# The node stage's first two weight loads issued in the last head pair ahead of the store of the inverse denominators

## The reference, cut to what matters

```python
xn = _layernorm(x)                                  # x: 1250 x 768
x = x + gnn(xn, edges, W, b) + mix(xn, w_qkv, w_proj)
x = x + ffn(_layernorm(x), ...)                     # 8 experts, top-1 routing

# mix: 12 heads of 64, attention with a polynomial in place of exp
A = einsum('bhnd,bhmd->bhnm', q, k)
numerator = 1.0 + A + 0.5 * A * A
attn = numerator / numerator.sum(axis=-1, keepdims=True)
out = einsum('bhnm,bhmd->bhnd', attn, v)            # then @ w_proj

# gnn: h = xn @ W, then the sum over edges (row -> col) of h[row] * norm
```

## Time and profile before

| | us |
|---|---|
| median of 3 runs | 1134.38 |
| lowest and highest of them | 1133.22, 1134.51 |
| the profiled execution, its own time | 1134.08 |
| its span in the trace | 1132.4 |
| outside the span (1134.08 - 1132.4) | 1.68 |

### The profile page before, as it was taken

One profiled execution on the slowest core, in us unless ns is written; L12 is line 12 of the kernel. 1 busy time (PEld: TensorE's weight loads), 2 busy tenths in 40 slices (PEclk: granted clock), 3 DMA queues, 4 the chain that ended last, 5 costly groups with the idle time before them and its releaser, 6 DMA issues.

```text
span 1132.4 us, 15230 instructions
## 1 busy us (share of the span) xinstructions
PE 931.7 (82%) x5250; PEld 886.2 (78%) x5250; DVE 733.0 (65%) x1396; ACT 459.4 (41%) x678; POOL 308.5 (27%) x201
## 2 busy tenths in 40 slices
PE   3896789989989989989896779699999963399970
PEld 3896688888878878878885679699999963399960
DVE  6877269879889788789786445464445436166633
ACT  2311266666666666666665212110101020266520
POOL 2035555535646545533452000000000004100004
PEclk9998899999999999999998889899999975599995
DMA  9966433373363454498534564736252332879978
GB/s 279 321 180 151 85 49 61 37 137 60 62 112 60 85 88 60 89 198 197 116 54 107 72 155 104 167 80 154 77 154 78 95 110 53 238 232 278 282 192 272
DMA packets 143091, 152.24 MB, mean 134 GB/s; under 512 B 72205, under 2 KB 119926, under 8 KB 142024
## 3 DMA queue, kind: packets, MB, share of 16 engines
q1 hardware_dynamic: 114213, 137.46, 46.7%
q0 software_dynamic: 28432, 14.05, 9.8%
q10 hardware_dynamic: 403, 0.17, 0.1%
HBM read 105.79 MB, written 46.78 MB: 135 GB/s over the span
## 4 chain that ended last, share of the span: by engine, by line
PE 57%; DVE 15%; ACT 9%; issue 8%; DMA 7%; POOL 2%; SPq 1%; DVEq 0%; ACTq 0%; POOLq 0%
PE ps L1770 14%; PE ps L1772 13%; PE ps L1771 13%; PE ps L1156 6%; PE ps L1140 3%; ACT Ph L802 3%; PE ps L1141 3%; ACT Pf L824 2%; DVE Pl L1014 2%; DVE Ph L1012 1%; DMA rows<-oE 1%; POOL rows L1511 1%; DMA Cs<-counts 1%; PE ps L1404 1%; PE ps L1116 1%
## 5 line engine op out<-in xcount | busy, mean ns | idle before, releaser
L363 POOL DMA_INDIRECT counts<-countc,idxu x157 | 273.4, 1741 | 308.5 <-DMA counts<-countc,idxu 229.9
L1014 DVE SCALAR_TENSOR_TENSOR Pl<-Pf,Ph 125x832 fp32r<-125x832 f32 (+1 forms) x180 | 184.3, 1026 | 72.6 <-ACT Ph L802 68.5
L824 ACT ACTIVATE Pf<-ps 125x832 f32<-125x832 f32 (+1 forms) x180 | 155.8, 866 | 145.9 <-PE ps L1141 140.6
L1156 PE MATMUL ps<-Ph,vsb 125*128 125x416 f32 (+1 forms) x360 | 132.1, 367 | 9.2 <-DVE Pl L1014 8.8
L1156 PE MATMUL ps<-Pl,vsb 125*128 125x416 f32 (+1 forms) x360 | 128.0, 356 | 0.0
L1511 POOL DMA_INDIRECT rows<-XF,slots x10 | 14.8, 1480 | 341.1 <-DVE slots L1626 338.4
L1770 PE MATMUL ps<-XH,wqkH 128*128 128x416 f32 (+1 forms) x216 | 81.6, 378 | 19.9 <-DVE R L932 10.2
L1770 PE MATMUL ps<-wH,XH 128*125 128x384 f32 x240 | 84.8, 353 | 9.9 <-DVE OHL L959 5.8
L1156 PEld LDWEIGHTS ps<-Ph,vsb 125*128 125x128 f32 x360 | 68.8, 191 | 19.9 <-DVE Pl L1014 9.5
L1771 PE MATMUL ps<-wL,XH 128*125 128x384 f32 x240 | 83.3, 347 | 0.0
L1772 PE MATMUL ps<-wH,XL 128*125 128x384 f32 x240 | 82.9, 346 | 0.0
(11 more groups left out here) (235 smaller groups left out, 2130.8 us busy)
## 6 DMA issues: line engine op xcount, KB each, us to landing
Cs<-counts SPq DMA_DIRECT2D x20, 546.9 KB
w1s<-L_ffn_w SPq DMA_DIRECT2D x8, 1152.0 KB, 8.6
w2s<-L_ffn_w SPq DMA_DIRECT2D x8, 1152.0 KB, 6.5
rows<-blank SPq DMA_DIRECT2D x2, 4215.0 KB
odram<-OHL SPq DMA_DIRECT2D x12, 625.0 KB, 8.9
oS<-odram SPq DMA_DIRECT2D x10, 750.0 KB, 4.8
vdram<-VS SPq DMA_DIRECT2D x10, 672.0 KB
vsb<-vdram SPq DMA_DIRECT2D x12, 560.0 KB
```

The costliest lines, as they stand in the source:

```text
L363: pool.indirect_dma_start(out=counts, out_offset=bass.IndirectOffsetOnAxis(ap=idxu[:, c:c + 1], axis=0), in_=countc[:, c:c + 1], in_offset ...
L824: act.activation(Pf[:, i % RING, :, 0:w], ps[0:T, 2 * (i % 2):2 * (i % 2) + 2, 0:w], ACT.Square, bias=1.0).then_inc(sq_done, 1)
L1014: dve.scalar_tensor_tensor(out=p, in0=f, scalar=1.0, in1=h.bitcast(F32), op0=ALU.add, op1=ALU.subtract).then_inc(p_lo, 1)
L1156: ins = pe.matmul(ps[:, 4 + s % 2, 0:w], vsb[:, 2 * kp + t, a, :], part[:, m % RING, t, 0:w], start=(kp == 0 and t == 0 and part is Ph), s ...
```

## The change

In the last pair's branch of SP's `turn`, the wait for `g_mm` (the last use of the tile kt that `wst3` lies over) and the loads of thirds 3 and 4 move ahead of `store_inverse`. The load of third 5 stays behind `load_inverse`. No instruction of another engine is touched, and no load is added.

```diff
                 else:
+                    sp.wait_ge(g_mm, PAIRS)
+                    load_w3(sp, 3)
+                    load_w3(sp, 4)
                     store_inverse(j)
                     load_inverse(j)
-                    sp.wait_ge(g_mm, PAIRS)
-                    for wc in (3, 4, 5):
-                        load_w3(sp, wc)
+                    load_w3(sp, 5)
```

## The result

| | before | changed |
|---|---|---|
| median, us | 1135.59 (1133.22 to 1139.6, 6 runs) | 1127.02 (1124.09 to 1129.24, 6 runs) |
| span of the profiled execution, us | 1132.4 | 1126.9 |
| inverses' store issued (L685), us | 594.66 | 596.23 |
| last output store issued (L734, now L735), us | 636.84 | 631.29 |
| **distance** between these two issues, us | 42.18 | 35.06 |

The ratio of the changed kernel to the one before is 0.9923, with a 95% interval of 0.9905 to 0.9940, that is 8.7 us less, and between 6.8 and 10.8. The forecast was 8.05 us. The kernel before was measured again beside the changed one, three runs more, and its median moved from 1134.38 to 1135.59, so the ratio says more than the difference of two medians. Later medians of the changed kernel, beside other runs of the one before, were 1125.29 and 1123.84.

What follows compares the result with a forecast made beforehand. The prediction took ACT's wait for W's third 3, felt by DVE and PE, as the bound; removing 8.05 us, all other terms zero, took the median from 1134.38 to 1126.3 us, range 1124.2 to 1128.3.

Steps and rivals of the forecast that it cites:

- The wait: ACT's 8.05 us wait for W's third 3 in the last head pair goes whole; DVE's falls to 2.6 us.
- DVE sets the pace: Behind the stall the stage is as long as DVE's unaltered work, busy 19.29 of 19.60 us.
- The clock: Behind the stall PE idles less than 1 us and should keep 2.4 GHz; counted as zero gain.
- the rival: PE, not DVE, holds the stage behind the stall; full clock makes the gain 11.2 us, 1123.2 us; chance 0.06.
- The third load: Third 5 lands with 0.7 us in hand; as rival, ACT waits 1.7 us at step 24, 1128.0 us, chance 0.07.
- What the early loads meet: Beside the KLB copy at 576 us, early loads delay the second head by zero, at most 0.8 us.
- a sign of being wrong: First scores of the second head starting later than 586.7 us would show the forecast wrong.
- the slower rival: KLB and the values' second half queue among early weights, delaying the second head; example 1138.4 us, chance 0.03.
- The scatters: POOL's long wait moves to between 576 and 584 us; 26.3 us stay in hand behind the last scatter.
- Behind the stage: From the output store on, everything moves earlier as a block; output store to first csum stays 20.3 us.
- given back: At the edge counts csum still starts near 657 us, so the time stays at 1134.4 us; chance 0.04.

Runs made afterwards that it cites:

- after: The first profiled execution of the changed kernel, traced against the kernel before; span 1126.9 us, ratio 0.9923 of before.
- again: The changed kernel run once more, unaltered; 0.9922 of the time of the kernel before.
- one_early: The changed kernel with only third 3 loaded ahead of the inverses' store, third 4 behind the rden loads as before; 0.9941 of the time before.
- again_more: The changed kernel run a third time, unaltered; 0.9924 of the time of the kernel before.
- crowd: The changed kernel with an unneeded 3.5 MB DRAM-to-DRAM copy issued between the KLB copy and the early loads; 0.9940 of the time before.
- keep_clock: The changed kernel with 4, 2 and 9 extra unused products before PE's waits at steps 21, 22 and 23 of the last pair; 0.9949 of before.
- round19: The changed kernel with ACT's three roundings of W at steps 19, 22 and 25 instead of 18, 21 and 24; 0.9922 of the time before.
- crowd_double: The changed kernel with two unneeded DRAM-to-DRAM copies, 7 MB, issued ahead of the early loads; 0.9997 of the time before.
- late_ask: The kernel before, loads unmoved, with ACT's three roundings at steps 23, 25 and 28 instead of 18, 21 and 24; 0.9965 of before.

## Why the prediction was right

**The wait.** The loads were issued at 577.75, 1.70 us after the forecast time, 1.65 of it because the whole trace is later there, landed with room (5.1 and 7.2 us), and the 8.05 us on ACT are gone. DVE's wait is 2.61 us, as worked out. In again, where no slow clock took anything back, the distance fell by 42.18 - 34.10 = 8.08 us, where 8.05 was forecast.

**DVE sets the pace.** Right, with the exception of the some 3 us of slow products in after; the table above and the busy shares are its evidence. one_early is the sharpest case: 2.52 us of waiting on ACT, 0.57 of it on the path.

**The clock.** Here a step was wrong. The prediction said that PE would idle less than 1 us and keep 2.4 GHz to 612. PE did idle only 0.69 us there, but eight microseconds later it waited 2.05 us for DVE, which was splitting third 3. In the trace of before this wait is 0.90 us (at 615.11), since PE had run at half clock until about 613 and came to it late; the prediction looked only at the first gap. The clock fell to half behind the longer wait. In after and again_more this cost 0.87 and 0.89 us on DVE, in crowd 0.66, in again nothing, and in one_early the clock didn't fall. So the term that was counted as zero measured 0 to 0.9 us, as a loss, where the rival had it as a gain of 3.15 us. That rival is refuted: with the clock at 1.00 throughout keep_clock gained 8.03 us in the stretch and not 11.2, and in again DVE stayed busy while PE was at half clock. (The 3.15 was also too much: a product starts every 0.35 us at half clock and every 0.19 at full, which is more than half.)

**The third load.** It landed in time in after, as forecast. round19 waited 0.67 us for it, without harm to the stage.

**What the early loads meet.** Forecast zero, with 0.8 as the bound; the first scores are 11.01 us behind the KLB copy's issue against 11.09. By the clock of the trace they started at 588.20, later than the 586.7 that the prediction named as a sign of being wrong; the sign was badly chosen, since all of that trace is 1.6 us late. crowd and crowd_double put 3.5 and 7 MB more in that place and did not move the scores, so the slower rival by that mechanism is refuted. Its other half was named wrong: enough early traffic does take the gain away, but through the weights' own landing. The inverses were read 29.2 us after their store (625.44 - 596.23) without a wait.

**The scatters.** The forecast of a long wait of POOL between 576 and 584 was wrong: the wait there was 2.79 us, and 3.11 at the same place before, so the two loads cost POOL nothing that can be seen, and the 6.87 us did not move there. The last scatter was issued at 620.11, not 608.14. POOL was behind already at 560 us, with 18 scatters to go instead of 14 after that time, so this isn't from the change. SP came to the counts at 636.86, 16.8 us later, where I had counted on 26.3 in hand.

**Behind the stage.** From the output store to the first csum it took 20.28 us before and 19.41 after. The same distance is 17.92 in again and 17.18 in again_more, so it varies by itself by more than 2 us. late_ask, which has SP's order of before, took 17.85, so that order alone isn't what made the 20.28; the kernel before itself was traced only once. From the output store to the span's end it was 495.56 and 495.61 us, and 493.59 and 492.48 in the two other traces of the changed kernel; nothing was given back. The ratios of the three measurements (0.9923, 0.9922, 0.9924) stand for 8.6 to 8.8 us, the stretch for 7.1 to 8.1. That lies within their intervals, and whether the difference is more than noise is open: behind the output store the traces of this study vary by 5 us.

**How much was luck.** The saving of 8.05 us holds by the traces. That the median itself fell within 0.7 us of the forecast 1126.3 is in part luck: the two later medians of the same kernel are 1125.29 and 1123.84, the second outside the range given, and the six runs of the kernel before spread over 6.4 us, where the prediction reckoned with 1.3.

## What to carry to other kernels

A DMA queue whose issuer waits is a queue in which a load can be late for no reason of its own: look at what the issuer was waiting for when a late load was issued, and move the load ahead of that wait if its buffer is free. Count a wait not where it stands but where the pacing engine feels it, since 2.5 us on ACT cost 0.6 here, while in late_ask a rounding in front of the wrong instruction cost DVE 2.2 us with every load in place. When a stall is removed, look at who paces the stage next and put the remaining work into that engine's holes; that gave 2.4 to 3.9 us more by the medians of this study.

## What the runs showed that I had not expected

The granted clock fell to half with no long gap in PE's work: in after its waits from 600 us on were 0.69, 0.90, 0.51 and 2.05 us, and it was busy for 2.03 of 4.00 us ahead of the fall; in again the waits before the fall were 0.69 and 0.90 us. The fall came at different places in executions of the same kernel (609 in after, 604 in again), so the stage's length varies between executions: 34.1 or 35.1 us. In one_early PE's waits were the same (0.68, 0.90, 0.53 and 2.04 us) and the clock didn't fall up to 620 us, so the waits alone don't tell whether it will. With products put into the waits (keep_clock) it didn't fall either, in the one trace taken. What decides the place, or whether it falls at all, isn't shown by these runs.

A load behind a DRAM-to-DRAM copy of 3.5 MB on the same queue landed after 16.5 us instead of 5.1, while the copy of KLB that was issued ahead of it took 3.3 us, as without it (3.2). The Trainium skill, "DMA: Bandwidth & Descriptors", section "Queues, rings and completion order", says that each DMA engine consumes one queue's descriptors in ring order and switches between queues at packet boundaries. The trace agrees with the first: the load landed at 594.4, 3.2 us after the copy (577.26 + 13.9 = 591.2). At what grain the engines switch no run here shows; the scatters of POOL, which the page of the profile lists on a queue of another kind, were not spared and waited 12.7 us in crowd and 20.0 us in crowd_double.
